# The recurrent mix of layer 2 as one pipeline over 64 state rows, its values spread through DRAM

## The reference, cut to what matters

```
xx = shift(x) - x                       # the token before, minus this one
m = tanh((x + xx * maa_x) @ w1)         # 4 groups of 32
m = einsum('btfd,fdc->fbtc', m, w2)     # mw, mk, mv, mr
xf = x + xx * (maa_f + m_f)             # f = w, k, v, r
r, k, v = xr @ W_r, xk @ W_k, xv @ W_v
w = exp(-exp(decay + tanh(xw @ dw1) @ dw2))
for t:                                  # per head; S is 16 x 16
    y[t] = r[t] @ (S + u * outer(k[t], v[t]))
    S = w[t] * S + outer(k[t], v[t])
y = (y - mean(y)) * rsqrt(var(y) + eps) * ln_g + ln_b
x = layernorm(x + y @ W_o)
```

## Time and profile before

| what | us |
|---|---|
| median of 3 runs | 2833.56 |
| lowest, highest | 2827.65, 2833.76 |
| the profiled execution | 2825.35 |
| its span | 2823.6 |
| mix of layer 2 in it, 2108 to 2332 | 224 |

### The profile page before, as it was taken

The page is one execution under the profiler, slowest core; times in us unless marked ns, Lnnn a source line. Parts: engine busy times, 40 slices in busy tenths (PEclk is TensorE's granted clock), DMA queues, the critical chain, the costliest instruction groups (busy, mean ns, idle before and its releaser), DMA issues. The chain is left out here.

```text
span 2823.6 us, 64040 instructions
## 1 busy us (share of the span) xinstructions
PE 2414.3 (86%) x25809; PEld 1592.7 (56%) x25861; DVE 2072.8 (73%) x3811; ACT 1585.3 (56%) x4088; POOL 264.2 (9%) x278
## 2 busy tenths in 40 slices
PE   6888888888888888888985999999987877999777
PEld 5676676666666776664433666666542322332376
DVE  6899999898999889982033777787626765885465
ACT  3566666666666666663243777777631113677344
POOL 0000000000000000000020110100002432110342
PEclk9999999999999999998996999999988998999889
DMA  5111111111101111102008999898310003220421
GB/s 187 32 33 32 24 25 32 32 32 32 32 21 29 32 32 32 32 2 71 0 22 218 232 234 240 228 249 226 95 38 0 0 0 107 70 76 17 176 69 65
DMA packets 205728, 219.50 MB, mean 78 GB/s; under 512 B 32966, under 2 KB 191447, under 8 KB 199991
## 3 DMA queue, kind: packets, MB, share of 16 engines
q1 hardware_dynamic: 203033, 210.44, 28.5%
q0 software_dynamic: 2400, 4.95, 0.5%
HBM read 137.96 MB, written 79.79 MB: 77 GB/s over the span
## 5 line engine op out<-in xcount | busy, mean ns | idle before, releaser
L2876 DVE TENSOR_REDUCE dl_ZO<-dl_XP 128x64 f32<-128x128 f32 (+6 forms) x448 | 219.8, 491 | 15.4
L1990 ACT ACTIVATE da_AB<-ps 128x384 f32<-128x384 f32 x256 | 124.5, 490 | 142.6 <-PE ps L1851 139.0
L2143 DVE TENSOR_TENSOR ps<-ps,da_window 128x192 f32<-128x192 f32 (+1 forms) x256 | 101.2, 395 | 118.3 <-PE ps L1874 114.0
L2451 PE MATMUL ps<-dl_ST,ident 128*128 128x512 f32 x416 | 187.9, 595 | 0.0
L2871 DVE TENSOR_TENSOR dl_XP<-dl_ZO,dl_G 128x128 f32<-128x128 f32 (+5 forms) x384 | 177.1, 461 | 13.2
L1470 DVE TENSOR_REDUCE ra_top<-ps 128x1 f32<-128x512 f32 x256 | 159.3, 680 | 36.3 <-PE ps L1236 22.8
L2000 ACT ACTIVATE da_E<-ps,da_top 128x512 f32<-128x512 f32 x256 | 176.1, 688 | 17.4 <-DVE da_top L2146 17.0
L2146 DVE TENSOR_REDUCE da_top<-ps 128x1 f32<-128x512 f32 x256 | 176.9, 691 | 8.8
L1370 ACT ACTIVATE ra_PT<-ps 128x512 f32<-128x512 f32 x256 | 135.9, 602 | 61.2 <-PE ps L1267 59.3
L1881 PE MATMUL ps<-ident,da_E 128*128 128x128 f32 x1024 | 168.9, 288 | 1.3 <-ACT da_E L2000 1.2
L2385 PEld LDWEIGHTS ps<-X,dl_taps_v 128*128 128x128 f32 x1088 | 141.4, 211 | 16.0 <-issue 10.7
(11 more groups left out here) (410 smaller groups left out, 5880.6 us busy)
## 6 DMA issues: line engine op xcount, KB each, us to landing
da_bands<-da_AB SPq DMA_DIRECT2D x128, 384.0 KB, 3.8
dl_Abc<-dl_ends SPq DMA_DIRECT2D x64, 512.0 KB, 6.4
da_window<-da_bands SPq DMA_DIRECT2D x128, 192.0 KB, 4.4
da_across<-da_bands SPq DMA_DIRECT2D x128, 192.0 KB, 4.4
da_parts<-da_split SPq DMA_DIRECT2D x64, 96.0 KB, 3.4
ra_parts<-ra_split SPq DMA_DIRECT2D x16, 384.0 KB, 3.7
rf_We<-in_rf_We SPq DMA_DIRECT2D x1, 4608.0 KB, 23.7
da_K<-da_parts SPq DMA_DIRECT2D x16, 256.0 KB
```

What stands on the lines that cost most here:

```text
L1990: eng.activation(AB[:, j % STAGES, h, :, :], ps[:, band_bank(v), 0:2 * BAND].rearrange("p (k x) -> p k x", k=2), ACT.Copy)\
L2451: eng.matmul(ps[:, UPDATES[r], :], c.ident[:, :], quarters[:, r, :, :], start=True, stop=alone)
L2876: link(eng.tensor_reduce(ZO[:, to:to + 1 + (2 * I - 1) * CH:CH].rearrange("p (k i) -> p k i", k=2), XP[:, :, :, SB - 1 - t:], AXX, ALU.add))
```

## The change

The scans, the preparation of the next batch and the norm of the last one become one sequence.

- The matrix rw_spread, its load, and the 64 products with it (L891) go. Instead SyncE writes a batch's values (128 x 512, 256 KB) to a DRAM buffer, waits for that, and reads them back repeated: 32 transfers for a batch, each a run of four value rows (8 KB) onto the 16 partitions of a head, 128 KB; 8 of them (one for each head) fill a piece of four j. They go to a new tile rw_KV, 128 x 2 x 16 x 512, double-buffered by batch.
- VectorE multiplies rw_KV by the keys in place (products), and the scan reads the product from there. So both operations now have both inputs in SBUF. The product for step j + 1 stands right behind step j's scan and what is put between, and in front of scan j + 1, which waits for it.
- The operations of preparation(b + 1) and norm(b - 1) are dealt out over the 16 steps of batch b, one or two to a step; each product on TensorE gets a bank of its own, and r, k, v, the decays and own values are double-buffered. centred gets its own tile (it was rS's first buffer).
- In the preparation the values come first: scale_mix and add_tokens of f = 2, then the projection of the values.
- ScalarE loads one table set by hand ahead of the norm's Ln and Exp (deviation).
- GpSimd's operation is the same, with the same inputs in SBUF.

```diff
-    BEHIND = 3
+    PIECE = 4
...
-        spread = c.sb("rw_spread", [P, HS, P], ctx)
...
-        rkv = c.sb("rw_rkv", [P, 3, T], ctx)
-        wd = c.sb("rw_wd", [P, T], ctx)
+        rkv = c.sb("rw_rkv", [P, 2, 3, T], ctx)
+        wd = c.sb("rw_wd", [P, 2, T], ctx)
...
+        KV = c.sb("rw_KV", [P, 2, HS, T], ctx)
...
+        values = [c.nc.dram_tensor(f"rw_values{e}", (P, T), F32, kind="Internal").ap() for e in range(2)]
...
+        @block.sync
+        def _(eng):
+            for b in range(B):
+                eng.wait_ge(act_done, b * ACTS + 2)
+                eng.dma_start(values[b % 2], rkv[:, b % 2, 1, :]).then_inc(stored, 16)
+                eng.wait_ge(stored, 16 * (b + 1))
+                if b:
+                    for q in range(HS // PIECE):
+                        eng.wait_ge(spread[q], 16 * HS // 2 * b)
+                if b >= 2:
+                    eng.wait_ge(scanned, (b - 1) * HS)
+                for q in range(HS // PIECE):
+                    for h in range(P // HS):
+                        rows = values[b % 2][HS * h + PIECE * q:HS * h + PIECE * (q + 1), :].rearrange("(o j) t -> o (j t)", o=1)
+                        eng.dma_start(KV[HS * h:HS * (h + 1), b % 2, PIECE * q:PIECE * (q + 1), :].rearrange("p j t -> p (j t)"),
+                                      rows.to_broadcast([HS, PIECE * T])).then_inc(spread[q], 16)
...
-                        eng.matmul(c.ps[:, spread_bank(j), :], spread[:, j, :], rkv[:, 1, :], start=True, stop=True).then_inc(vb_ready, 1)
...
+            def sums(b, j):
+                if j == 0 and b >= 2:
+                    eng.wait_ge(yo, 2 * b - 3)
+                eng.wait_ge(read, b * HS + j + 1)
+                eng.matmul(c.ps[:, b % 2, :], gather[:, j, :], rS[:, j % DEEP, :], start=j == 0, stop=j == HS - 1).then_inc(summed, 1)
...
+            mixes(0, 2, 1, 3, 0)
+            project(0, 1, 5)
+            project(0, 0, 8)
+            project(0, 2, 9)
+            decay_down(0)
+            decay_up(0)
+            own_weights(0)
...
+                eng.preload_act_table_set("natural_log_exp_and_others")
...
-                    eng.wait_ge(scanned, b * HS + j + 1)
-                    if j >= DEEP:
-                        eng.wait_ge(summed, b * HS + j - DEEP + 1)
-
-                    eng.tensor_tensor(rS[:, j % DEEP, :], rkv[:, 2, :], S[:, j % DEEP, 0:T], ALU.mult).then_inc(read, 1)
+                    g = b * HS + j
+                    eng.wait_ge(act_done, b * ACTS + 4)
+                    eng.wait_ge(scanned, g + 1)
+                    if g >= DEEP:
+                        eng.wait_ge(summed, g - DEEP + 1)
+                    eng.tensor_tensor(rS[:, j % DEEP, :], rkv[:, b % 2, 2, :], S[:, j % DEEP, 0:T], ALU.mult).then_inc(read, 1)
...
-            def states(b):
-                for j in range(HS + 1):
-                    if j < HS:
-                        eng.wait_ge(vb_ready, b * HS + j + 1)
-                        eng.tensor_tensor(c.ps[:, spread_bank(j), :], rkv[:, 0, :], c.ps[:, spread_bank(j), :], ALU.mult).then_inc(kv_ready, 1)
-                    if j >= 1:
-                        k = j - 1
-                        eng.wait_ge(kv_ready, b * HS + k + 1)
-                        if k >= DEEP:
-                            eng.wait_ge(read, b * HS + k - DEEP + 1)
-                        eng.tensor_tensor_scan(S[:, k % DEEP, 1:], wd[:, :], c.ps[:, spread_bank(k), :], 0.0,
-                                               ALU.mult, ALU.add).then_inc(scanned, 1)
...
+            def products(b, j):
...
+                eng.wait_ge(spread[j // PIECE], 16 * HS // 2 * (b + 1))
+                eng.tensor_tensor(KV[:, b % 2, j, :], rkv[:, b % 2, 0, :], KV[:, b % 2, j, :], ALU.mult).then_inc(keyed, 1)
+
+            def scan(b, j):
+                g = b * HS + j
+                eng.wait_ge(act_done, b * ACTS + 7)
+                eng.wait_ge(keyed, g + 1)
+                if g >= DEEP:
+                    eng.wait_ge(read, g - DEEP + 1)
+                eng.tensor_tensor_scan(S[:, j % DEEP, 1:], wd[:, b % 2, :], KV[:, b % 2, j, :], 0.0, ALU.mult, ALU.add).then_inc(scanned, 1)
...
+            scale_mix(0, 2, 2)
+            scale_mix(0, 1, 3)
...
+            products(0, 0)
...
+                following, tail = b + 1 < B, b > 0
+                for j in range(HS):
+                    scan(b, j)
+                    if following and j == 0:
+                        shift(b + 1)
+                    if tail and j == 2:
+                        sum_up(b - 1)
+                    if following and j == 3:
+                        scale_mix(b + 1, 2, 2)
+                        scale_mix(b + 1, 1, 3)
+                    if tail and j == 4:
+                        centre(b - 1)
+                    if following and j == 4:
+                        add_tokens(b + 1, 2, 3)
+                    if following and j == 5:
+                        scale_mix(b + 1, 3, 4)
+                        scale_mix(b + 1, 0, 5)
+                    if following and j == 6:
+                        add_tokens(b + 1, 1, 4)
+                        add_tokens(b + 1, 3, 6)
+                    if following and j == 7:
+                        add_tokens(b + 1, 0, 7)
+                    if following and j == 9:
+                        own_keys(b + 1)
+                    if tail and j == 11:
+                        scale_norm(b - 1)
+                    if tail and j == 12:
+                        shift_norm(b - 1)
+                    if following and j == 13:
+                        own_values(b + 1)
+                    if tail and j == 15:
+                        residual(b - 1)
+                    if b * HS + j + 1 < B * HS:
+                        products((b * HS + j + 1) // HS, (j + 1) % HS)
```

More of the change, by code:

```diff
@@ L870, in four_mixes, with project, decay_down @@
                        .then_inc(pe_done, 1)
[L872 removed]
+            def project(b, n, ready):
+                eng.wait_ge(chain, b * STEPS + ready)
+                eng.matmul(c.ps[:, 3 + n, :], Wrkv[:, n, :], mix[:, 1 + n, :], start=True, stop=True).then_inc(pe_done, 1)
+            def decay_down(b):
                 eng.wait_ge(chain, b * STEPS + 10)
[L874 to L884 removed]
@@ L983, in shift, with scale_mix @@
                 eng.scalar_tensor_tensor(xxx[:, :], xx[:, :], maa[:, 0:1], x(b), ALU.mult, ALU.add).then_inc(chain, 1)
-            def scale_mixes(b):
-                for f in range(4):
-                    eng.wait_ge(pe_done, b * PES + 2 + f)
-                    eng.scalar_tensor_tensor(mix[:, f, :], c.ps[:, f, :], maa[:, 1 + f:2 + f], xx[:, :], ALU.add, ALU.mult).then_inc(chain, 1)
-            def add_tokens(b, f):
-                eng.wait_ge(chain, b * STEPS + 6)
+            def scale_mix(b, f, at):
+                eng.wait_ge(pe_done, b * PES + at)
+                eng.scalar_tensor_tensor(mix[:, f, :], c.ps[:, 3 + f, :], maa[:, 1 + f:2 + f], xx[:, :], ALU.add, ALU.mult).then_inc(chain, 1)
@@ L992, in add_tokens, with own_keys @@
+            def add_tokens(b, f, after):
+                eng.wait_ge(chain, b * STEPS + after)
                 eng.tensor_tensor(mix[:, f, :], mix[:, f, :], x(b), ALU.add).then_inc(chain, 1)
+            def own_keys(b):
+                eng.wait_ge(act_done, b * ACTS + 4)
+                eng.scalar_tensor_tensor(ruk[:, :], rkv[:, b % 2, 2, :], maa[:, 6:7], rkv[:, b % 2, 0, :], ALU.mult, ALU.mult).then_inc(chain, 1)
             def own_values(b):
+                eng.wait_ge(pe_done, b * PES + 11)
+                eng.tensor_tensor(we[:, b % 2, :], rkv[:, b % 2, 1, :], c.ps[:, 6, :], ALU.mult).then_inc(chain, 1)
@@ L1062 @@
+            sum_up(B - 1)
+            centre(B - 1)
+            scale_norm(B - 1)
+            shift_norm(B - 1)
+            residual(B - 1)
 HEADS = 16
```

196 lines of the change are left out of this document (105 added, 91 removed).

## The result

The changed kernel takes 2853.4 us (median of 6 runs, 2847.36 to 2862.58) against 2833.16 of the kernel before in the same comparison: ratio 1.0065, interval 1.0042 to 1.0088. Timed once more beside the kernel before it gave 1.0051 (1.0033 to 1.0068). So it is 0.5 to 0.65% slower; 2842 was forecast, with 2813 to 2858 as its range.

What follows compares the result with a forecast made beforehand. VectorE was taken to bound the scan blocks and a chain over three engines the gaps. Loop +10.5, start 0 and end +1.4 gave +12 us on a mean of 2830.1: 2842 us, range 2813 to 2858.

Steps and rivals of the forecast that it cites:

- The turns: In scans and products, two-input SBUF operations of VectorE and GpSimd's SBUF reading exclude each other; the second stands until the first ends.
- plain step: Scan's end to scan's end with only a key product between: 2.71 us instead of 1.71, bounds 1.86 and 3.03.
- dealt-out work: Preparation and norm operations put between the scans: 6.08 us per preparation, 2.1 per norm, 24.2 us in all.
- The loop: First scan's start to last scan's end: 196.1 us against 185.65, +10.5.
- The start: Before the first scan, values projected, stored and read back: -2.5 to +2.8 us, taken as 0.
- The end: From the last scan's end to R, 13.9 us before: +1.4 us (-1.3 to +1.4).
- The table load: In the end, the load ahead of Exp goes, saving 1.28 us.
- the clock's term: In the end, TensorE at a lower clock for last adding up, mean and variance: 3 x 0.9 = +2.7 us.
- Values late: Rival: VectorE stands before products 0, 4, 8, 12 if 128 KB transfers take 1.5 us or more; 2890 us, chance 0.05.
- scan takes no turns: Rival: the scan leaves GpSimd room, other two-input operations still take turns; step 1.86, 2815 us, chance 0.11.
- no turns at all: Rival: VectorE and GpSimd never exclude each other on SBUF; stretch 149 us, 2792 us, chance 0.05.
- dearer turns: Rival: both engines pay their whole duration at each turn; 3.03 us a step, +20 more, 2862 us, chance 0.05.

Runs made afterwards that it cites:

- old_scan_sbuf: Kernel before with only the key product moved from PSUM to an SBUF tile, so the scan has both inputs in SBUF: ratio 1.016 to the kernel before.
- the second profile: The changed kernel, unchanged, profiled and timed again beside the kernel before: ratio 1.0051, scans' stretch 201.1 us.

## Why the prediction was right, and where it was off

- **The turns hold for the scan**, the step on which the sign hung. Forecast 2.71 us for a plain step, measured 2.68; a step with one addition 3.57 for 3.42, two additions 4.00 for 4.02, one PSUM operation 3.08 for 3.05, own_keys 3.46 for 3.42. Without GpSimd's reading it is 1.90 (1.86 said), and with the scan's input put into SBUF in the old kernel 2.34 (2.33 said). The Trainium skill gives this rule for any VectorE instruction with two SBUF inputs against a GpSimd one that reads SBUF (SBUF — State Buffer, Who interferes with whom); by that rule, the runs agree for the scan too, and for a GpSimd copy with one input, and they agree that a GpSimd fill, which only writes, makes no turn.
- **The step that was mis-sized is the dealt-out work**: 24.2 us in the sum, 30.7 measured (200.8 - 1.23 - 63 x 2.68). It was rightly named in kind, but nearly each kind cost more than forecast. Steps with an addition or scale_norm took 0.15 to 0.21 more: half of the 0.15 is GpSimd's product, 1.26 in these steps and not 1.18, and most of the rest the scan, which starts 0.09 behind its product and not 0.04. The residual took 3.26 to 3.63 for 3.05. Centre with an addition took 3.87 and, with the mean 2.1 us late from TensorE, 5.28, for 3.63; the last centre, which the sum put beside an addition, stood alone (3.26). The loop came to +15.2 for +10.5. The late mean also answers a sentence of the prediction: that inside a batch TensorE's slower product still fits a step. It did not in the third batch. The window of that batch, the 10 us around the place, and the centre that waited:

```profile
2235.71:2290.04 54.33, 40.39 (x61) 12.31 (x60) 50.42 (x50) 7.52 (x11) 21.53 (x16) 0.72 0.63 83
2242.00:2252.00 10.00, 10.00 (x18) 3.17 (x18) 7.75 (x10) 0.38 (x1) 3.62 (x3) 0.60 0.00 0
...
2250.90 0.69 DVE L1091 TENSOR_TENSOR rw_centred<-rw_Y,ps 128x512 f32<-128x512 f32 x1 [2.07 <-PE ps L917]
```

TensorE is busy all through those 10 us at 0.60. The prediction had named ScalarE as the engine that might be late.
- **The start**: 0 forecast, +0.4 measured, and +0.8 in the second profile. A wait of 5.4 us for transfers stood in it, which smaller transfers later took away.
- **The end**: +1.4 forecast, -0.4 and, in the second profile, -0.6 measured. The table load went as said, 1.28. The lower clock was there in the batch (0.62) but TensorE was granted 1.00 from 2332 to 2338, so the last adding up and the mean took 1.13 as before and only the variance paid, 2.02: 0.9 of the 2.7. The sum of the end had the clock's term three times too large.
- **Values late**: no wait at pieces 4, 8 and 12. They landed at 127 to 135 GB/s over a batch, 1.0 us for 128 KB. The estimate from the Trainium skill's figures had been 1.2 (SBUF — State Buffer, Door 1: The DMA port swizzle); the measurement decides, and by either there was no wait.
- The rival *scan takes no turns* (2815) is refuted by the records of 1.94 and 2.12 and by old_scan_sbuf; *no turns at all* (2792, a stretch of 149 us) is refuted by the same records, and only the kernel without GpSimd's reading comes near it, with 153.2; *dearer turns* (3.03) is refuted by 2.68.
- The median is 11.4 us above the forecast. 3.2 of it are the mix (+15.2 for +12), in which errors partly cancel: +6.5 for the dealt-out work, -1.9 for 63 steps of 2.68 and not 2.71, +0.4 for the start, -1.8 for the end. Of the rest, 3.1 are the base (I added to the mean of four executions, 2830.1, and the kernel before has 2833.2 here), and 5.0 are what the medians of this comparison differ by beyond the mix. In the second comparison that is 1.9. That these three parts lie on the same side is chance.
- One reading of the prediction mixes two lines: GpSimd's operation at 1476.15 is of L2068 (median 1152, longest 1261 ns), and the 1367 of the earlier trace rows is that of an earlier operation, of L2057 (from 1473.69). What was read from them, that GpSimd pays too when it comes second, is borne out by its record of 1.40 to 1.57 us in plain steps, where it takes 1.09 to 1.26 alone.

## What to carry to other kernels

Before a tile moves from PSUM to SBUF, look at who else reads SBUF then: if VectorE's operation gets a second SBUF input while GpSimd reads SBUF, expect each such step to grow with the length of GpSimd's operation (here by 0.23 us for 0.61, by 0.71 for 1.09 and by 0.89 for 1.26). A copy of a long-lived operand into PSUM by an idle engine (here 2 copies for 32 operations) buys the overlap back: 160.0 us for 200.8. And deal out work in a way that leaves late results a step or two of slack, for TensorE above all: where it had less to do in a step it was granted 0.62 to 0.82 instead of 1.00, and single products took up to 2.08 us for 1.13 just where others waited for them.
